# AdaLN block with distance attention and a mixture of experts: the output projection's stage loop with one step less between a tile group's normalisation and its turning

## The reference, cut to what matters

```python
x = x + ga * _L0_attn_ref(h, ...)               # ctx @ Wo + bo, gated
h = _layernorm(x, axis=-1) * (1 + cb) + sb
...
scores = jax.nn.softmax(xf @ gate_w.T, axis=-1)  # xf is h, 4096 x 256; 8 experts
vals, idx = jax.lax.top_k(scores.T, k)           # k = 512 tokens for each expert
```

## Time and profile before

| | us |
|---|---|
| median of 3 runs | 1500.56 (1499.22 to 1502.44) |
| the profiled execution, its time | 1500.56 |
| the profiled execution, its span | 1498.7 |
| PE busy | 1432.0 (96%) |
| DVE busy | 1200.0 (80%) |
| ACT busy | 1060.1 (71%) |
| POOL busy | 935.7 (62%) |

### The profile page before, as it was taken

One profiled execution on the slowest core, in us unless ns is written; L12 is line 12 of the kernel. 1 busy time (PEld: TensorE's weight loads), 2 busy tenths in 40 slices (PEclk: granted clock), 3 DMA queues, 4 the chain that ended last, 5 costly groups with the idle time before them and its releaser, 6 DMA issues.

```text
span 1498.7 us, 44334 instructions
## 1 busy us (share of the span) xinstructions
PE 1432.0 (96%) x16334; PEld 1130.3 (75%) x16334; DVE 1200.0 (80%) x3693; ACT 1060.1 (71%) x2293; POOL 935.7 (62%) x1549
## 2 busy tenths in 40 slices
PE   6989999999999999999999999999999658999997
PEld 4556888888888888888888888888888546676675
DVE  6959999999999999999999999999979794223222
ACT  3558888889888898888988888888886850112211
POOL 4348787877878777787778777787785003234222
PEclk9999999999999999999999999999999757999999
DMA  7364121221212222122221222212344514345331
GB/s 241 131 211 129 35 63 37 76 65 49 63 36 74 58 58 63 36 71 75 72 63 35 66 54 71 64 34 65 91 140 126 169 66 156 88 97 161 96 81 21
DMA packets 100065, 126.88 MB, mean 85 GB/s; under 512 B 30133, under 2 KB 81445, under 8 KB 97801
## 3 DMA queue, kind: packets, MB, share of 16 engines
q1 hardware_dynamic: 92394, 113.06, 25.7%
q0 software_dynamic: 6480, 9.29, 3.3%
q10 hardware_dynamic: 974, 1.71, 0.3%
HBM read 93.83 MB, written 30.16 MB: 83 GB/s over the span
## 4 chain that ended last, share of the span: by engine, by line
PE 84%; DVE 6%; ACT 3%; issue 3%; DMA 1%; POOL 1%; SPq 1%; POOLq 0%; DVEq 0%; another core or an unknown queue 0%
PE pbank L956 27%; PE pbank L971 18%; PE pbank L942 15%; PE pbank L1421 7%; PE pbank L1431 7%; PE pbank L621 2%; DVE region_x L1034 2%; PE pbank L1275 2%; ACT region_x L1002 1%; PE pbank L636 1%; ACT region_c L997 1%; PE pbank L1336 1%; DVE region_p L1600 1%; PE pbank L1322 1%; PE pbank L603 1%
## 5 line engine op out<-in xcount | busy, mean ns | idle before, releaser
L942 PE MATMUL pbank<-region_s 128*128 128x512 bf16 (+3 forms) x1280 | 400.0, 349 | 4.2 <-DVE maxima L1034 3.5
L956 PE MATMUL pbank<-ident,region_a 128*128 128x128 f32 x2048 | 328.7, 274 | 2.9
L956 PE MATMUL pbank<-ident,region_x 128*128 128x128 f32 x2048 | 329.4, 273 | 0.9 <-POOL region_x L1074 0.9
L1066 POOL TENSOR_SCALAR region_x<-region_x,maxima 128x1664 f32<-128x1664 f32 (+3 forms) x128 | 202.4, 1581 | 174.6 <-ACT region_x L1002 171.4
L956 PEld LDWEIGHTS pbank<-ident,region_a 128*128 128x128 f32 x2048 | 254.9, 141 | 41.8 <-ACT region_c L997 10.2
L1034 DVE CUSTOM_DVE_ANT_0 region_x<-pbank,region_t,maxima 128x512 f32<-128x512 f32 (+1 forms) x416 | 269.1, 698 | 16.6 <-PE pbank L942 16.6
L956 PEld LDWEIGHTS pbank<-ident,region_x 128*128 128x128 f32 x2048 | 252.1, 141 | 28.7 <-ACT region_o L997 6.5
L997 ACT ACTIVATE region_p<-pbank 128x512 f32<-128x512 f32 x384 | 224.2, 608 | 67.5 <-PE pbank L956 67.4
L997 ACT ACTIVATE region_o<-pbank 128x512 f32<-128x512 f32 x448 | 266.5, 618 | 0.2
L1002 ACT ACTIVATE region_x<-region_x 128x384 f32<-128x384 f32 (+1 forms) x512 | 246.8, 508 | 0.0
L1034 DVE CUSTOM_DVE_ANT_0 region_a<-pbank,region_t,maxima 128x512 f32<-128x512 f32 (+1 forms) x352 | 230.5, 693 | 18.3 <-PE pbank L942 18.3
(11 more groups left out here) (219 smaller groups left out, 2347.7 us busy)
## 6 DMA issues: line engine op xcount, KB each, us to landing
region_t<-factor_rows SPq DMA_DIRECT2D x16, 1024.0 KB, 5.4
region_s<-q_split SPq DMA_DIRECT2D x256, 64.0 KB, 2.3
region_s<-k_split SPq DMA_DIRECT2D x256, 64.0 KB, 2.3
region_x<-in_fc_t SPq DMA_DIRECT2D x16, 1024.0 KB, 8.1
q_split<-region_o SPq DMA_DIRECT2D x16, 384.0 KB, 2.6
k_split<-region_t SPq DMA_DIRECT2D x16, 384.0 KB, 2.7
heads_out<-region_o SPq DMA_DIRECT2D x256, 16.0 KB, 1.5
region_c<-heads_out SPq DMA_DIRECT2D x16, 256.0 KB, 4.5
```

Source lines behind the costliest of these rows:

```text
L942: nc.tensor.matmul(score_ps[bank_of(s)][:, 0:(hi - lo) * P], stacks[:, b, 0, t * P:(t + 1) * P], stacks[:, b, 1, lo * P:hi * P], start=Tru ...
L956: last = nc.tensor.transpose(turn_ps[(h * NR + j) % TB][:, q * P:(q + 1) * P], rows[t][:, k * P:(k + 1) * P], ident[:, :])
L1066: nc.gpsimd.tensor_scalar(row, row, maxima[:, 4, n:n + 1], 1.0, ALU.add, ALU.mult).then_inc(shifted_pool, 1)
```

## The change

The turning and all that follows it come one step earlier. PE turns group s - 1 at step s (before, s - 2), does the gate matmuls of group s - 2 (before, s - 3) and the transpose back of group s - 3 (before, s - 4). ACT applies h2t to the same group whose z it has just written, in the same step, and saves the logits of group s - 2. DVE copies the logits of group s - 3. The loops are one step shorter on each engine. No instruction is added or removed, only the order on PE, ACT and DVE changes.

```diff
     def tensor_stage(pe):
-
-        for s in range(G + 4):
+        for s in range(G + 3):
...
-            if 0 <= s - 2 < G:
-                g = s - 2
+            if 0 <= s - 1 < G:
+                g = s - 1
                 pe.wait_ge(z_done, g + 1)
...
-            if 0 <= s - 3 < G:
-                g = s - 3
+            if 0 <= s - 2 < G:
+                g = s - 2
                 pe.wait_ge(h2t_done, KC * (g + 1))
...
-            if 0 <= s - 4:
-                g = s - 4
+            if 0 <= s - 3:
+                g = s - 3
                 pe.wait_ge(gate_saved, g + 1)
...
     def scalar_stage(act):
...
-        for s in range(G + 3):
+        for s in range(G + 2):
             if 0 <= s - 1 < G:
                 g = s - 1
...
                 last.then_inc(z_done, 1)
-            if 0 <= s - 2 < G:
-                g = s - 2
                 if g == 0:
                     act.wait_ge(gt_done, B)
                 for k in range(KC):
                     act.wait_ge(z_turned, KC * g + k + 1)
...
-            if 0 <= s - 3 < G:
-                g = s - 3
+            if 0 <= s - 2 < G:
+                g = s - 2
                 act.wait_ge(gate_mm, g + 1)
...
     def vector_stage(dve):
...
-        for s in range(G + 4):
+        for s in range(G + 3):
...
-            if 0 <= s - 4 < G:
-                logits(s - 4)
+            if 0 <= s - 3 < G:
+                logits(s - 3)
```

## The result

The changed kernel takes 1508.61 us (median of 5 runs, 1507.85 to 1512.67) against 1500.56 us before; the ratio is 1.0056 with an interval of 1.0044 to 1.0067. It is slower by 8 us, as forecast in direction and mechanism; the forecast was 10.0 us. One execution of the fourth experiment's kernel took 2937 us where its nine others took 1492 to 1496; the ratios leave it out.

What follows compares the result with a forecast made beforehand. The prediction took PE to bound the stage loop at 5.15 us a stage, with z late after the change. Late projection 7 8.1, drain 0.2 and clock in the fill 1.7 gave 10.0 us on 1500.56: 1510.6 us, range 1506 to 1515.5.

Steps and rivals of the forecast that it cites:

- What bounds the loop: Stage loop: PE alone fills 5.15 us a stage before; afterwards z of group 4 would be 2.6 us late.
- The fill: First projections: PE waits for the first z, so projections 2, 3 and 4 start 3.8, 5.0 and 6.1 us late.
- the steady state: Later stages: a dependence over two stages takes 11.81 us against 10.30, making projection 7 8.1 us late.
- The signs: New profile: turnings wait for z nearly every stage, last projection ends near 1174, last logits 8 to 10 us later.
- The drain: After the last projection: 0.67 us saved at z, 0.87 lost to group 7's turning at 1.2 GHz; +0.2 us.
- the clock term in the fill: First wait for z: clock drops, costing 0.87 us at group 0's turning plus a quarter of projection 2; 1.7 us.
- Half clock through the loop: Rival: shorter waits hold PE at 1.2 GHz, a stage's PE work doubles to 10.3 us; 1531 us, chance 0.04.
- Only the fill stalls: Rival: z's wait is paid once, then PE keeps 5.15 us a stage; +4.0, 1504.6 us, chance 0.07.
- Absorbed: Rival: z is in time, moved work only delays the last projection; +1.0, 1501.6 us, chance 0.04.
- Faster by a shorter drain: Rival: PE's new order costs nothing and the drain shortens at full clock; up to -3.4, 1497.2 us, chance 0.03.

Runs made afterwards that it cites:

- fourth experiment: Changed kernel, but PE turns tiles of the early-loaded modulation gates in place of z and does not wait for z: loop 47.3 us, ratio 0.9995.
- ninth run: Changed kernel measured again, unchanged, on one chip with the kernel before: 1509.32 against 1502.12 us, ratio 1.0050, loop 56.6 us.
- tenth: Kernel before the change, profiled once more on the same chip as the ninth run: loop 47.9 us, 323.1 us behind it.
- experiments one: Changed kernel with PE's gate and back of earlier groups placed ahead of the turning that waits for z: ratio 1.0055, loop 55.5 us.
- two: Changed kernel with DVE's reciprocal and product of a group moved right behind its variance: ratio 1.0036, loop 54.7 us.
- three: Changed kernel with both gate and back ahead of the turning and DVE's reciprocal and product earlier: ratio 1.0035, loop 52.2 us.
- six: Changed kernel with ACT's order put back as before, so only PE's and DVE's order changed: ratio 1.0072, loop 58.5 us.
- eighth experiment: Kernel of experiment three with the turning of group 0 held back until behind projection 2: ratio 1.0079, loop 56.0 us.

## Why the prediction was right, and which term was off

**What bounds the loop.** Right: before, PE alone, 5.15 us a stage; after, z, which comes too late for its new place. With that wait taken away (fourth experiment) projection 7 is 7.0 of its 8.8 us earlier.

**The fill and the steady state.** Counted from the first projection, projections 2 to 7 start 3.6, 5.1, 6.0, 7.4, 7.4 and 8.8 us later than before, where the forecast had 3.8, 5.0, 6.1, 6.6, 7.6 and 8.1. The fill came as summed: 17.4 us to projection 3 (1146.65 - 1129.27 expected, 1145.96 - 1128.58 measured). For a pair I expected 11.81 us and got 11.76 from projection 5 to 7. From projection 3 to 5 it was 12.57. Of the 0.81 more, 0.6 are two small DVE operations on that stretch of the chain (L1554 and L1534), which took 0.49 and 0.46 us where their neighbours take 0.17 and 0.16, and 0.2 are projection 3 itself (3.67 against 3.47), as the row of 3.65 in the earlier trace rows had it. POOL was busy while the two ran (L1748 to L1753, 1151.64 to 1155.38); whether that slowed them was not tested. The circle over two stages was tested by three edits that leave PE's amount of work alone, and each moved the pair by about what the sum said: -0.81 (said 0.82), -0.92 (said 1.0), +0.90 (said 0.8).

**The signs.** PE waited for z in six of eight turnings, and the last projection ended at 1173.76, as said. The waits at the turnings of groups 3 to 6 were not 0.4 to 1.1 us each but 1.2 us and nothing in turn. The last logits came 7.5 us later, a little under the 8 to 10. The granted clock near 1140 to 1143 was 1.00, not 0.50: the drop that 1510.6 counts on was not in this profile.

**The drain.** I expected +0.2 and it came to -0.6. From the end of projection 7 to the maximum it was 1177.09 - 1165.63 = 11.46 before, and is 1184.59 - 1173.76 = 10.83 now. The saving at z is as said: the turning begins 0.05 us after z ends (1179.17, 1179.22), against 0.81 before. The turning ran at 1.2 GHz, also as said, but cost 0.54 more (1.77 us against 1.23), not 0.87. The rest, from the turning's end to the maximum, is 0.4 shorter, because in this profile the clock came back before the last logits; in the profile before it was still at 0.50 then.

```profile
1180.00:1182.00 2.00, 2.00 (x22) 1.15 (x20) 0.00 (x0) 1.55 (x2) 0.00 (x0) 0.50 0.00 0
...
1183.10:1185.00 1.90, 1.46 (x19) 1.21 (x12) 0.93 (x5) 1.55 (x2) 0.00 (x0) 1.00 0.00 0
```

The two clock parts belong to the execution. In the ninth run the turning took 1.09 us, the clock fell behind it and stayed low up to the last logits (4.0 us from the turning's end to the maximum, as before), and the drain was 10.6 us. In the tenth, the kernel before, the turning took 1.94 us, the clock came back (3.4 us), and the drain was 11.6. What repeats is the saving of 0.76 at z: the drain gains 0.6 to 1.0, and the 0.87 of the sum stands for a cost that appeared in one of two profiles.

**Where luck helped.** Without the clock term in the fill the sum gives 8.1 + 0.2 = 8.3 us, and the loop of the profiled execution has 8.2. Two errors cancel in that: 0.7 too little at projection 7 and 0.8 too much in the drain.

**The clock in the fill.** This is the term that was mis-sized: 1.7 us. The wait was there (2.51 us). Six profiles have this wait and PE's same order up to projection 2 (the kernel after, and experiments one, two, three, six and nine); the clock dropped in two of them, one and nine. These two have the longest waits, 2.54 and 2.68 us against 2.44 to 2.52, but 2.52 and 2.54 are so close that six profiles can't say whether the length decides. Where the clock dropped, the turning of group 0 still ran at full clock (1.09 and 1.15 us), and projection 2 took 1.6 to 1.7 us more; I had put half of the 1.7 into each. In the ninth 1.0 was left at projection 3 and 0.8 at projection 7. I added a delay at one place to the sum as if it passed through to the end. By these profiles the term should have been 0 to 0.8.

**Half clock through the loop.** The Trainium skill (TensorE: Matmul & The Clock Gate, section on HAM oscillation) describes a loop in which PE waits 3 to 5 us for data in every round and is throttled in every one. Inside this loop no wait is so long, so that case did not bear on the stages. In the kernel after, the wait of 2.51 us and those of 0.43 to 1.23 left the clock at 1.00; the drain's 3.78 is of that length, and there the clock fell. Shorter waits are no safe ground either: in the eighth experiment it fell around two waits of 1.47 and 1.99 us with 0.6 us of work between them, while in the sixth single waits of up to 1.60 us between projections left it alone. The rival of half clock throughout fell.

**The other rivals.** "Only the fill stalls" is what the third experiment's kernel does, and there 4.4 us remain; in the changed kernel the pairs of stages cost the rest. "Absorbed" is nearest to the fourth, with 1.8 us at projection 7. "Faster by a shorter drain" has its gain in the rows, 0.6 us, an order below the price.

## What to carry to other kernels

Before taking a stage out of a software pipeline, compare the end of the producer with the time at which the consumer would now stand in its engine's queue. If it is late, follow the dependence until it closes, here over two stages and three engines, and compare that sum with the same number of stages of the engine that is the limit. The difference, times the number of rounds, is one part of the loss. The other is what the first groups lose until the circle has closed once; here it was the larger, 5.0 of 8.8 us, and of it 4.4 stayed when the circle was made short enough. The wait is best filled with work that is ready (gate and back, 0.8 us a pair here), and a delay at one place must be followed to the end of the loop before it is added.

## What was not expected of the hardware

The same program, with a first wait of 2.68 us on PE in one execution and 2.51 in another, had its granted clock at 0.50 behind it in the one and at 1.00 in the other. In the drain it was the other way round: behind 3.64 us the turning took 1.09 us, behind 3.78 us 1.77. The kernel before has the same spread, 1.23 and 1.94 us behind waits of 2.22 and 2.35. So one profile can't decide what a wait of this size costs: projection 2 took 5.08 us in the one and some 3.5 in the other.
